# Loads and stores of a conv pair spread at two blocks per TensorE step, with SyncE held to TensorE's pace

## The reference

```python
# layer 0: a position bias, the same for all x
nd = log(|c * rel| + 1) / (log(|c * pos| + 1) + EPS)     # rel = tril(t - s), pos from the row
y = x + (relu(nd[..., None] * W1 + b1) @ W2 + b2)        # 32 hidden units to 16 channels
# layer 1: every position mixes its 16 channels, by a matrix of its row plus one of its column
ret = einsum(y, w + eye)
ret += rank-2 product of qw1[t], qw2[t] + diag qdd[t]    # depends on the row t
ret += rank-2 product of kw1[s], kw2[s] + diag kdd[s]    # depends on the column s
```

## Time and profile before

| | us |
|---|---|
| median of 3 runs | 977.46 (973.42 to 980.99) |
| the profiled execution | 958.2 |
| its span, first to last instruction | 956.4 |

### The profile page before, as it was taken

One profiled execution on the slowest core, in us unless ns is written; L12 is line 12 of the kernel. 1 busy time (PEld: TensorE's weight loads), 2 busy tenths in 40 slices (PEclk: granted clock), 3 DMA queues, 4 the chain that ended last, 5 costly groups with the idle time before them and its releaser, 6 DMA issues.

```text
span 956.4 us, 39070 instructions
## 1 busy us (share of the span) xinstructions
PE 751.1 (79%) x18210; PEld 551.5 (58%) x18210; DVE 451.8 (47%) x482; ACT 386.0 (40%) x412; POOL 369.8 (39%) x204
## 2 busy tenths in 40 slices
PE   0687465897779857879899989987979679997972
PEld 0255344675657545656557656756557456766972
DVE  7495332375336533456336534553336334662342
ACT  3969223543545415633434335332433334431200
POOL 4545212232223312326456637553446445650000
PEclk9879777899889987989999989998899899998997
DMA  6785587838982999378964998399835996297089
GB/s 135 178 173 106 123 155 159 193 80 202 233 186 58 216 161 196 91 143 188 249 139 82 231 204 177 62 210 187 188 77 112 234 218 149 54 202 148 5 188 168
DMA packets 364286, 149.64 MB, mean 156 GB/s; under 512 B 97372, under 2 KB 363996, under 8 KB 364124
## 3 DMA queue, kind: packets, MB, share of 16 engines
q1 hardware_dynamic: 226528, 80.00, 41.5%
q10 hardware_dynamic: 137596, 67.14, 30.9%
HBM read 77.61 MB, written 69.47 MB: 154 GB/s over the span
## 4 chain that ended last, share of the span: by engine, by line
PE 54%; SPq 14%; DMA 9%; issue 8%; ACTq 6%; DVE 4%; ACT 4%; POOL 0%; DVEq 0%
PE main L679 22%; PE main L668 18%; PE bias L693 14%; SPq L296 9%; DMA mats_a<-a_mats 7%; SPq L287 5%; ACTq L239 5%; DMA homes<-in_x 2%; ACT homes L440 1%; ACT hidden L429 1%; DVE homes L260 1%; ACT homes L456 1%; DVE homes L574 1%; DMA out_mixed<-homes 1%; DVE w_blocks L549 1%
## 5 line engine op out<-in xcount | busy, mean ns | idle before, releaser
L393 POOL TENSOR_TENSOR hidden<-log_table,row_scale 128x1024 f32<-128x1024 f32 x192 | 365.7, 1919 | 486.8 <-PE bias L693 481.1
L679 PE MATMUL main<-homes,mats_b 32*32 32x120 f32 (+1 forms) x9216 | 283.7, 272 | 84.0 <-issue 59.8
L429 ACT ACTIVATE hidden<-hidden,b_col 128x1024 f32<-128x1024 f32 x192 | 219.0, 1148 | 316.6 <-issue 156.4
L679 PEld LDWEIGHTS main<-homes,mats_b 32*32 32x32 f32 x9216 | 256.5, 133 | 151.4 <-issue 113.8
L668 PE MATMUL main<-homes,mats_a 32*32 32x128 f32 x8192 | 267.5, 280 | 63.1 <-DMA mats_a<-a_mats 35.2
L668 PEld LDWEIGHTS main<-homes,mats_a 32*32 32x32 f32 x8192 | 242.3, 131 | 124.1 <-issue 79.2
L592 DVE SCALAR_TENSOR_TENSOR homes<-bias,b_col,homes 64x512 f32<-64x512 f32 (+1 forms) x256 | 185.9, 747 | 134.1 <-PE bias L693 84.9
L693 PE MATMUL bias<-hidden,w_blocks 128*64 128x512 f32 x768 | 211.0, 655 | 24.8 <-ACT hidden L429 15.3
L574 DVE TENSOR_TENSOR homes<-main,homes 128x1024 f32<-128x1024 f32 x128 | 156.8, 1225 | 137.2 <-PE main L668 134.6
L564 DVE COPY homes<-main 128x960 f32<-128x960 f32 x64 | 74.1, 1158 | 211.2 <-PE main L679 211.1
L456 ACT ACTIVATE homes<-main 128x960 f32<-128x960 f32 (+1 forms) x80 | 71.0, 890 | 136.6 <-PE main L679 118.1
(11 more groups left out here) (36 smaller groups left out, 30.1 us busy)
## 6 DMA issues: line engine op xcount, KB each, us to landing
out_mixed<-homes ACTq DMA_DIRECT2D x208, 192.0 KB
homes<-in_x SPq DMA_DIRECT2D x200, 192.0 KB, 6.5
homes<-in_x SPq DMA_DIRECT2D x72, 256.0 KB, 7.1
out_mixed<-homes ACTq DMA_DIRECT2D x64, 256.0 KB
out_mixed<-homes ACTq DMA_DIRECT2D x72, 128.0 KB, 4.5
homes<-in_x SPq DMA_DIRECT2D x136, 64.0 KB
mats_a<-a_mats SPq DMA_DIRECT2D x256, 32.0 KB
b_mats<-homes SPq DMA_DIRECT2D x2, 512.0 KB, 3.4
```

The costliest lines, as they stand in the source:

```text
L393: nc.gpsimd.tensor_tensor(hidden_tile(u, g).rearrange("p (j s) -> p j s", j=ROWS), bass.AP(logs.tensor, logs.offset, [list(logs.ap[0]), [1 ...
L429: nc.scalar.activation(hidden_tile(u, g), hidden_tile(u, g), ACT.Relu, bias=b1_col[:, 0:1])\
L679: mm = pe.matmul(main[of_group(g), i % 2, j * W:j * W + REGION_TILES[k] * ROWS], b_weights(g, C * ROWS + j), y_column(k, g, C * ROWS + j), ...
```

## The change

- SP waits at every step until PE has finished the step before (`main_ready`), and walks through all steps, the column steps too.
- The five first pieces of region r are issued two blocks per step, from steps 8, 12, 16, 20 and 24 counted from the first row step of region r - 2 (`LOAD_STEPS`, `since_rows`). Steps 15 and later of this count are the column steps of region r - 1. The last piece goes with four blocks per step at T = 8 and 9 (6 and 7 in region 0). The waits for `out_done` stay, ahead of a piece's first block.
- The stores of a piece go two blocks per step, four steps per piece, and a piece starts after the one before it has been issued: at T = 2, 6, 10 and 14, and from step 18 of the count, which is the third column step of the next region. In the last region it is four blocks per step.
- `bias_step` starts at step 3 instead of 1. For a region of 15 tiles the tiles 0 to 14 have the steps 3, 4, 6, 8, 10, 12, 14, 16 and then, as before, 17, 19, 21, 23, 25, 27, 29 (before: 1, 3, 5, 7, 9, 11, 13, 15, 17 and so on). ACT adds the constant one bias step later than PE makes the tile.

```diff
@@ -28,7 +28,10 @@
 HOMES = 3
 STORE_PIECES = {8: (2, 3, 3), 15: (2, 3, 3, 3, 4)}
 LOAD_PIECES = {8: (1, 3, 4), 15: (1, 3, 3, 3, 4, 1)}
-PORTIONS = (3, 3, 2)
+STORE_SHARE = 2
+LOAD_SHARE = 2
+LAST_LOAD_STEP = {8: 6, 15: 8}
+LOAD_STEPS = (8, 12, 16, 20, 24)
...
@@ -166,7 +169,7 @@
 
         def bias_step(k, T):
 
-            return 1 + T * (COL_TILES + REGION_TILES[k] - 3) // (REGION_TILES[k + 1] - 1)
+            return 3 + T * (COL_TILES + REGION_TILES[k] - 5) // (REGION_TILES[k + 1] - 1)
...
-        def portions_at(k, s):
+        def blocks_of(part, share):
+            return BLOCK_ORDER[part * share:(part + 1) * share]
+
+        def store_share(k):
+
+            return STORE_SHARE if k + 1 < REGIONS else BLOCKS // 2
+
+        def store_start(k, i):
+
+            ready = piece_start(store_pieces(k), i + 1)
+            return ready if i == 0 else max(ready, store_start(k, i - 1) + BLOCKS // store_share(k))
+
+        def since_rows(r, k, s):
+
+            return s - COL_TILES + (COL_TILES + REGION_TILES[r] if k == r + 1 else 0)
+
+        def stores_at(k, s):
 
             found = []
-            for r, step in ((k - 1, s + REGION_TILES[k - 1] if k else -1), (k, s - COL_TILES)):
-                if r < 0:
-                    continue
-                for i in range(len(store_pieces(r))):
-                    p = step - piece_start(store_pieces(r), i + 1)
-                    if 0 <= p < len(PORTIONS):
-                        found.append((r, i, p))
+            for r in (k - 1, k):
+                if r >= 0:
+                    for i in range(len(store_pieces(r))):
+                        part = since_rows(r, k, s) - store_start(r, i)
+                        if 0 <= part < BLOCKS // store_share(r):
+                            found.append((r, i, part))
+            return found
+
+        def loads_at(k, s):
+
+            found = []
+            for r in (k + 1, k + 2):
+                if 2 <= r < REGIONS:
+                    for i, start in enumerate(LOAD_STEPS):
+                        part = since_rows(r - 2, k, s) - start
+                        if 0 <= part < BLOCKS // LOAD_SHARE:
+                            found.append((r, i, part))
             return found
...
-            def load_x(k, i):
+            def wait_slots(k, i):
                 T, n = piece_start(load_pieces(k), i), load_pieces(k)[i]
                 if k >= 1 and T + 1 >= HOME_TILES:
...
@@ -282,10 +308,13 @@
                 elif k >= 2 and T + 1 < REGION_TILES[k - 2]:
                     left = piece_of(store_pieces(k - 2), min(T + n, REGION_TILES[k - 2] - 1))
                     sp.wait_ge(out_done[left], times(STORE_PIECES, left, k - 2) * PER_PIECE)
+
+            def load_x(k, i, blocks):
+                T, n = piece_start(load_pieces(k), i), load_pieces(k)[i] * ROWS
                 t0 = tile_of(k, T) * ROWS
-                for b in BLOCK_ORDER:
-                    sp.dma_start(home_rows(b, x_slot(k, T), n * ROWS),
-                                 x[0, :, t0:t0 + n * ROWS, b * W:(b + 1) * W]).then_inc(x_in[i], DMA)
+                for b in blocks:
+                    sp.dma_start(home_rows(b, x_slot(k, T), n),
+                                 x[0, :, t0:t0 + n, b * W:(b + 1) * W]).then_inc(x_in[i], DMA)
...
-            loaded = [3, 5] + [0] * (REGIONS - 2)
             for k in range(REGIONS):
-
-                while k + 1 < REGIONS and loaded[k + 1] < 5:
-                    load_x(k + 1, loaded[k + 1])
-                    loaded[k + 1] += 1
                 if k == 2:
...
@@ -347,15 +371,23 @@
...
-                for T in range(REGION_TILES[k]):
-                    v, last = divmod(tile_of(k, T), CHUNK_TILES)
-                    if last == CHUNK_TILES - 1 and v + A_RING < CHUNKS:
-                        load_mats_a(v + A_RING)
-                    if k + 1 < REGIONS and T == min(6, REGION_TILES[k] - 4):
-                        load_x(k + 1, 5)
-                    if k + 2 < REGIONS and T in (7, 10, 13):
-                        load_x(k + 2, loaded[k + 2])
-                        loaded[k + 2] += 1
+                for s in steps(k):
+                    T = s - COL_TILES
+
+                    sp.wait_ge(main_ready, b_tile(k, s) if T < 0 else a_tile(k, T))
+                    if T > 0 or (s == 0 and k):
+                        v, last = divmod(tile_of(k, max(T, 0)) - 1, CHUNK_TILES)
+                        if last == CHUNK_TILES - 1 and v + A_RING < CHUNKS:
+                            load_mats_a(v + A_RING)
+                    if k + 1 < REGIONS and T in (LAST_LOAD_STEP[REGION_TILES[k]], LAST_LOAD_STEP[REGION_TILES[k]] + 1):
+                        part = T - LAST_LOAD_STEP[REGION_TILES[k]]
+                        if part == 0:
+                            wait_slots(k + 1, 5)
+                        load_x(k + 1, 5, blocks_of(part, BLOCKS // 2))
+                    for r, i, part in loads_at(k, s):
+                        if part == 0:
+                            wait_slots(r, i)
+                        load_x(r, i, blocks_of(part, LOAD_SHARE))
...
                 for s in steps(k):
-                    for r, i, p in portions_at(k, s):
-                        if p == 0:
+                    for r, i, part in stores_at(k, s):
+                        if part == 0:
                             taken, count = emptied(a_tile(r, piece_start(store_pieces(r), i + 1) - 1))
                             act.wait_ge(taken, count)
-                        for b in portion_blocks(p):
+                        for b in blocks_of(part, store_share(r)):
                             store_block(act, r, i, b).then_inc(out_done[i], DMA)
...
@@ -481,15 +513,19 @@
                     if T is not None:
                         if T + 1 < REGION_TILES[k + 1]:
                             make_hidden(tile_of(k + 1, T + 1))
-                        add_const_bias(k + 1, T)
-            for i in range(len(store_pieces(REGIONS - 1))):
-                for p in range(len(PORTIONS)):
-                    if piece_start(store_pieces(REGIONS - 1), i + 1) + p >= REGION_TILES[REGIONS - 1]:
-                        if p == 0:
-                            taken, count = emptied(a_tile(REGIONS - 1, piece_start(store_pieces(REGIONS - 1), i + 1) - 1))
+                        if T:
+                            add_const_bias(k + 1, T - 1)
+                        if T + 1 == REGION_TILES[k + 1]:
+                            add_const_bias(k + 1, T)
```

More of the change, by code:

```diff
@@ L327, in _ @@
             for i in range(3):
-                load_x(1, i)
+                load_x(1, i, BLOCK_ORDER)
             save_mats("a")
-            load_x(1, 3)
+            load_x(1, 3, BLOCK_ORDER)
             sp.wait_ge(mats_out["a"], 2 * DMA)
@@ L483, in _ @@
                             make_hidden(tile_of(k + 1, T + 1))
[L484 to L489 removed]
+                        if T:
+                            add_const_bias(k + 1, T - 1)
+                        if T + 1 == REGION_TILES[k + 1]:
+                            add_const_bias(k + 1, T)
+            last = REGIONS - 1
+            for i in range(len(store_pieces(last))):
+                for part in range(BLOCKS // store_share(last)):
+                    if store_start(last, i) + part >= REGION_TILES[last]:
+                        if part == 0:
+                            taken, count = emptied(a_tile(last, piece_start(store_pieces(last), i + 1) - 1))
                             act.wait_ge(taken, count)
[L491 to L492 removed]
+                        for b in blocks_of(part, store_share(last)):
+                            store_block(act, last, i, b).then_inc(out_done[i], DMA)
         @block.vector
```

12 lines of the change are left out of this document (4 added, 8 removed).

## The result

The change takes 993.39 us in the median of 4 runs (988.97 to 999.51), the kernel before 975.44 (4 runs, 965.03 to 980.99): the medians are 18 us or 1.8% apart. That the change is slower is shown, as the two ranges don't meet; by how much, between 1.8 and some 4%, is not. The profiled execution takes 989.29 us, its span 987.5. Forecast were 912 and a gain; the time lies 3 us above the range, in the part that the late-x rival named.

What follows compares the result with a forecast made beforehand. PE, busy 751.1 of 956.4 us, was taken as the bound, losing 137.5 us in regions 2 to 7 at transfer bursts. Savings 13 + 47.5 + 3 = 63.5 us gave 894.7 profiled, 912 median; range 868 to 990.

Steps and rivals of the forecast that it cites:

- late-x rival: Column step 7 of each region: PE waits for DVE, which waits for tile 1's x; 990 to 1005 us median, chance 0.19.
- These losses ...: 7 (upper) and 11 (lower): Steps 12 to 21 from the first row step, two loads and two stores each: 7 us lost per upper region, 11 per lower.
- slow work: Slower work behind PE's stalls: 1 us in each of regions 2 to 7, 2 us in region 1.
- What is left of 'issue' I put at 2: PE's mid-tile stops without a visible wait, 63.4 us before: 2 us left in each of regions 2 to 7.
- stalls of issue stay: Rival: PE's 63.4 us of mid-tile stops stay, in proportion to instructions, not bursts; 948 us median, chance 0.12.
- Late x of tiles 1 to 3: Before column step 7 of regions 2 to 7: x issued later costs 1 us per upper region, 3 per lower.
- Row matrices, "I keep 2": PE's waits for row matrices in regions 2 to 7, about 4 us per region before: 2 kept.
- Region 1, 13 us less: Region 1: paced loads leave planned stalls of 9, 5 and 2 us; 92 to 93 us instead of 105.4.
- Region 8, "3 us" less: Region 8: ACT's stores at the start are spread, PE has no bias there; 3 us less.
- The start and SP's wait, nothing: Region 0's later last load: nothing, 2 us at most; SP's wait per step: no cost.
- theory E: Follow-up theory, regions 2 to 7: bytes the DMA engines carry set the time, pacing only moves stalls; no chance given.
- the forecast's own range: Whole kernel, without rivals: 870 to 945 us, chance 0.52; upper end from 1.05 us per 192 KB.

Runs made afterwards that it cites:

- small_both: The change with stores of regions 1 to 7 and loads of regions 3 to 8 cut to an eighth of their rows: 831.86 us, 0.8765 of the kernel before.
- experiment 5: The change plus 12 transfers of 192 KB per region in regions 2 to 7; as stores: 970.43 us in column steps 10 to 15, 980.97 in row steps 0 to 5.
- spread: The change with one load per step in the crowded steps, later pieces three per step, and later bias steps: 967.67 us, 1.0211 of the kernel before.
- extra_cols: The change plus 12 HBM-to-HBM copies of 192 KB per region in column steps 10 to 15, regions 2 to 7: 1163.35 us, 1.2254 of the kernel before.
- bias_later: The change with bias tiles computed at column steps 6, 7, 9 and on instead of 3, 4, 6: 957.25 us, 1.010 of the kernel before.
- stores_paced: The kernel before with only the change's new stores, two blocks per step: 966.53 us, 1.0232 of the kernel before.
- loads_paced: The change with the old stores (3, 3 and 2 blocks in three steps): 956.59 us, 1.0118 of the kernel before.
- sp_free: The change without SP's wait for PE in each step: 957.0 us, 1.0114 of the kernel before.

## Why the prediction was wrong, by its steps

- **"These losses ...: 7 (upper) and 11 (lower)", the price of the crowd, is the step that failed.** It priced four transfers per step by the time of the DMA engines and of ACT alone and took the loss outside them as gone. But pacing doesn't remove bytes: it took 12 MB of the 48 from beside the row steps and put 10.6 beside the column steps. Over small_both's 251.2 us the column steps of regions 2 to 7 lose 120 us, where the terms of the prediction for them came to 60 (bursts 50, late x 10), 78 with all of "issue" and slow work. Before, the same difference was 81.5 us, and 35.8 in the row steps (over 260.2), at nearly the same mean DMA share, 0.75 and 0.76: the loss was in the columns to begin with, and the step should have asked what more bytes do there. The extra stores of experiment 5 say that it is not any column step, as the late ones took 14 MB for 6 us. Why the early ones lose more than the rows give back, 26 us against 16 on the other chips, stays open: thinning them out (spread) did not help.
- **"What is left of 'issue' I put at 2" failed with it.** It was 83.1 us from 150 to 850 against 63.4 before. The reading of "issue" as instructions late behind traffic fits (over a whole span 24 us in small_both, 107.5 in the change, 238 in extra_cols), but not that it goes when bursts are spread. The rival "stalls of issue stay" had the number nearer and the wrong reason, since it had them independent of the traffic.
- **Late x of tiles 1 to 3, "I take 1 and 3"**: 24.2 us in three regions, in place of 10. The rival's mechanism was right, with issues at 1.42 us each against its 1.16 to 1.3 and a DVE wait of 18 us, but it had 14 us in each of six regions; its total was met because "issue" rose with it: the agreement of 993.39 with its 990 to 1005 is luck in part. I had taken 0.65 to 0.8, medians of the whole kernel, for the fullest steps of all. As a cause of the loss it was only a share: bias_later takes it away and gains 6 us of some 16.
- **Row matrices, "I keep 2"**: right. 8.8 us are 1.5 per region, against 27.7.
- **Row steps**: no number was forecast for them alone, the direction was right. They fell from 296.0 to 282.0, and region 4's run without a stall for four pairs, (549.73 - 527.07) / 4 = 5.67 us each, as in the earlier trace rows:

```profile
527.07 1.94 PE L729 MATMUL bias<-hidden,w_blocks 128*64 128x512 f32 x8
...
549.73 1.94 PE L729 MATMUL bias<-hidden,w_blocks 128*64 128x512 f32 x8
```

- **Region 1, 13 us less: wrong**, +2.4. Its planned stalls came almost as computed, 11.30 us before step 7 (I took 9) and 3.18 before step 13 (I took 5), and the columns fell from 61.3 to 57.2 us. The waits inside its column steps come to 15.9 us, so some 5 of their 57.2 are slow work where I had 2. The row steps rose from 44.1 to 50.6 where I had them without a stall. Region 3's paced loads start in them, and they carry 183 GB/s at a DMA share of 0.84 where they had 158 at 0.75; but the same kernel took 44.7 and 48.5 there on two other chips, so this is not shown as the cause.
- **Region 8, "3 us" less**: its column steps took 37.0 us instead of 33.7. Stores that are spread meet more of its steps (37.5 us in stores_paced, 33.2 in loads_paced), but spread has them too and took 33.8.
- **The start and SP's wait, nothing**: right, -1.8 us, and sp_free.
- **The range** reached 990 and 993.39 came. The ratio of 1.020 between profiled execution and median did not carry over: it is 1.004 here. It was the odd execution of the kernel before, 958.2 where four others took 965 to 981, at the same mean clock, 0.913, as the change's 0.914; why it was so fast is open.
- **The sums**: region 1's terms, 9 + 5 + 2 + 2, are 18 us, not 20, so 91 us and not 92 to 93. The loss before, by the windows of its regions, is 31 us in a lower region and 19 in an upper one, not 33 and 18. And 7 us more in each of six regions put the upper end of the forecast's own range at 955, not 945. None of these moves the forecast by more than 2 us, nor does any explain the miss.

Open is also why parts of 1.2 to 2.3% don't add to more than 1.6% on the other chips; theory E would have it so, but the intervals, one per cent each, can't tell.

## What to carry to other kernels

Before you pace transfers, tabulate bytes, DMA share and lost time of each phase: pacing moves bytes, and what the lighter phase gives back the heavier one can take, with interest. Price a queue in the steps where both lists meet by the issue times of a full DMA, not by the medians of the whole kernel, and treat PE's "issue" stalls as part of the traffic's price: here they went only when bytes went. Compare medians with medians before you explain a size: a single profiled execution can lie 2% off its kernel's others. When one wait is taken away, look for what was hidden behind it before you count it as gained.

## What the runs showed that was not expected

- A copy of 192 KB from HBM to HBM in rows of 512 bytes took 16.2 us to land in the median and up to 33.8; stores of the same bytes 5.4 us. 14 MB of such copies cost 187 to 199 us over the change's 964, 14 MB of stores 6 to 16.
- With such copies PE stood up to 15.6 us between two matmuls of one tile, without a semaphore to wait for.
- The kernel before took 975.44 us in the runs of the result and 946 to 951 on five other chips, 3% less; the change took 993.39 there and 963 to 965 on two of the others, 3% less too.
